# Block-sparse attention in a four-layer fp32 kernel: scores in two halves over 64 rows, queries in two masked forms, full-width transposes

## The reference

```python
Q = heads(x @ W_Q); K = heads(x @ W_K); V = heads(x @ W_V)      # 16 heads of 8 channels
avg_sc = einsum(block means of Q, block means of K), averaged   # blocks of 32 tokens
_, idx = top_k(avg_sc, 3)                                       # 3 key blocks for each query block
logits = einsum('bhtqd,bhtknd->bhtqkn', Qb, Kb[:, :, idx]) / sqrt(8)
P = softmax(logits, axis=-1)                                    # over 3 * 32 = 96 keys
O = einsum('bhtqs,bhtsd->bhtqd', P, Vsel)
```

## Time and profile before

| what | value |
|---|---|
| time, median of 3 runs | 3850.96 us (3844.62 to 3856.63) |
| profiled execution, its own time | 3863.93 us |
| its span, first to last instruction | 3862.0 us |
| busy share of the span: PE, DVE, ACT, POOL | 87%, 60%, 44%, 14% |
| mean granted TensorE clock, share of full speed | 0.895 |
| HBM traffic over the span | 18 GB/s |
| the stage `block_attention` | about 269 to 594 us |

### The profile page before, as it was taken

The page is one execution under the profiler, slowest core; times in us unless marked ns, Lnnn a source line. Parts: engine busy times, 40 slices in busy tenths (PEclk is TensorE's granted clock), DMA queues, the critical chain, the costliest instruction groups (busy, mean ns, idle before and its releaser), DMA issues. The chain is left out here.

```text
span 3862.0 us, 124868 instructions
## 1 busy us (share of the span) xinstructions
PE 3363.0 (87%) x55256; PEld 2074.3 (54%) x55256; DVE 2329.7 (60%) x6283; ACT 1703.4 (44%) x3930; POOL 528.0 (14%) x532
## 2 busy tenths in 40 slices
PE   5866765789999999999989869999999999999985
PEld 2335552335555555455555425666666666666772
DVE  5756663277767777676774115666566666666545
ACT  3657773464444444344332325334444444343323
POOL 1213231000000000000000002222222222222210
PEclk9987677898989889899888879999999999999867
DMA  2000000121111111111000010000000000000000
GB/s 93 0 19 2 1 2 16 59 65 44 46 38 43 42 40 46 35 46 30 19 3 3 1 46 2 2 3 3 2 3 3 3 3 2 3 2 2 3 2 24
DMA packets 37035, 77.16 MB, mean 20 GB/s; under 512 B 7696, under 2 KB 11152, under 8 KB 35472
## 3 DMA queue, kind: packets, MB, share of 16 engines
q1 hardware_dynamic: 36496, 69.17, 5.5%
HBM read 64.83 MB, written 4.33 MB: 18 GB/s over the span
## 5 line engine op out<-in xcount | busy, mean ns | idle before, releaser
L1602 ACT ACTIVATE g_hidden<-ps 128x512 f32<-128x512 f32 x224 | 133.2, 594 | 405.3 <-PE ps L1460 405.1
L1460 PE MATMUL ps<-w_w 128*128 128x512 f32 x448 | 271.3, 690 | 42.7 <-DVE w_w L1810 27.0
L1316 PEld LDWEIGHTS ps<-g_Q,g_K 32*32 32x32 f32 x12288 | 192.6, 113 | 189.0 <-issue 127.3
L2279 PE MATMUL ps<-d_hp,d_w_k 128*128 128x512 f32 x512 | 283.7, 641 | 0.0
L1476 PE MATMUL ps<-g_hidden,w_w 128*128 128x512 f32 x448 | 257.3, 661 | 0.8 <-issue 0.7
L2357 POOL TENSOR_TENSOR d_sq<-d_QK 128x512 f32<-128x512 f32 x128 | 133.1, 1040 | 869.7 <-ACT d_QK L2408 708.4
L2377 ACT ACTIVATE d_F<-ps 128x128 f32<-128x128 f32 x256 | 70.8, 276 | 355.6 <-PE ps L2188 352.4
L1316 PE MATMUL ps<-g_Q,g_K 32*32 32x32 f32 (+1 forms) x12288 | 223.0, 218 | 4.0 <-issue 2.0
L791 ACT ACTIVATE att_p<-ps,att_mx 128x96 f32<-128x96 f32 x512 | 166.0, 361 | 74.6 <-DVE att_mx L736 70.1
L1284 POOL COPY g_xb<-X 128x512 f32<-128x512 f32 x8 | 6.9, 868 | 1191.5 <-DVE X L1822 1091.2
L2552 DVE SCALAR_TENSOR_TENSOR d_conv<-ps,w_conv_q,d_conv 128x511 f32<-128x511 f32 (+2 forms) x192 | 142.3, 741 | 34.1 <-ACT d_conv L2402 30.3
(11 more groups left out here) (502 smaller groups left out, 7877.1 us busy)
## 6 DMA issues: line engine op xcount, KB each, us to landing
w_w<-gate_rows SPq DMA_DIRECT2D x56, 256.0 KB, 3.4
w_w<-in_c_fc_dram SPq DMA_DIRECT2D x56, 256.0 KB, 4.0
w_w<-in_c_proj_dram SPq DMA_DIRECT2D x56, 256.0 KB, 2.8
X<-in_x_dram SPq DMA_DIRECT2D x1, 2048.0 KB, 8.3
w_c_fc<-in_c_fc_dram SPq DMA_DIRECT2D x1, 2048.0 KB, 12.7
w_c_proj<-in_c_proj_dram SPq DMA_DIRECT2D x1, 2048.0 KB, 17.1
ex_root<-gate_rows SPq DMA_DIRECT2D x1, 2048.0 KB, 13.8
h_rows<-k SPq DMA_DIRECT2D x1, 2048.0 KB, 6.3
```

Source lines behind the costliest of these rows:

```text
L1316: ins = e.matmul(later(scored, n_), keys_, queries(n_, planes, r_, 4 * i + j), start=(turn_ == 0 and part == 0 and n_ != 1), stop=(part == 1),
L1460: e.matmul(P[2], fc[:, n % 2, ts(f, C)], hs[n % 2], start=True, stop=True).then_inc(pe.steps, pe.did(now(f"u{i}")))
L1602: e.activation(r[:, slot], P[2], ACT.Relu).then_inc(act.steps, act.did(now(f"r{i}")))
L2279: ins = e.matmul(b, w_k[:, j, ts(H, C)], hp_of(u)[:, j:j + T], start=(j == 0), stop=(j == TAPS - 1))
```

## The change

Scores, maxima and the release of the score banks go by halves. Half h of a unit now has two matrices of scores for each sequence, each from 64 rows (two groups): the queries of the group that is not wanted are masked to zero. For that, `att_qx` becomes two tiles: form 0 keeps the even groups (made by DVE), form 1 the odd ones (made by POOL, `later_queries`), and the scales are a 128 x 8 table. The number of score matmuls stays 16 for a unit; they use two row tiles of 64 rows in place of four of 32. `scores(n+1, half)` waits only for the exponentials of the same half of unit n. The order of PE's and DVE's loops changes. `att_p` gets 128 columns for each matrix, the last 32 zeroed once by DVE, so that the transposes have a 128-column stationary operand. The rings hold three blocks in place of four. The slots of a unit hold the groups in the order 0, 2, 1, 3 (`group_of`).

```diff
...
@@ -668,15 +668,15 @@
 
 
     nc = k.nc
-    NK, BLOCKS, RING = 96, T // 32, 4
+    NK, BLOCKS, RING = 96, T // 32, 3
     UNITS = 2 * BLOCKS
     with ExitStack() as s:
         kg = k.sb("att_kg", [C, RING, B, NK], stack=s)
         vg = k.sb("att_vg", [C, RING, B, NK], stack=s)
-        qx = k.sb("att_qx", [C, RING, B, 4, 32], stack=s)
+        qx = [k.sb(f"att_qx{i}", [C, RING, B, 4, 32], stack=s) for i in range(2)]
         mx = k.sb("att_mx", [C, 2, 16], stack=s)
         den = k.sb("att_den", [C, 2, 16], stack=s)
-        p = k.sb("att_p", [C, 2, 16, NK], stack=s)
+        p = k.sb("att_p", [C, 2, 16, C], stack=s)
         pt = k.sb("att_pt", [NK, 2, 16, C], stack=s)
         vt = k.sb("att_vt", [NK, 2, 4, C], stack=s)
         o = k.sb("att_o", [C, 4, 32], stack=s)
@@ -684,6 +684,8 @@
         scored = k.ps[:, 0:4, 0:4 * NK].rearrange("p g (n k) -> p g n k", k=NK)
         BANK_VT, BANK_PT, BANK_O = 4, 5, 7
         place_of = lambda n: (n // 2, n % 2)
+        group_of = lambda j: 2 * (j % 2) + j // 2
+        scale_of = lambda half, i: k.w["pair_scale"][:, 4 * half + i:4 * half + i + 1]
         last_of = lambda q: 2 * q + 1
         pe, act, dve, pool, dma = k.stage("attention")
         with nc.Block() as block:
@@ -701,46 +703,56 @@
                         j = e.value_load(idx_row[0:1, bass.ds(q * 3 + i, 1)], min_val=0, max_val=15)
                         e.tensor_copy(vg[:, q % RING, :, ts(i, 32)], v1[:, :, bass.ds(j * 32, 32)]).then_inc(pool.steps, pool.did(f"v{q}"))
 
+                def later_queries(q):
+                    if q >= RING:
+                        e.wait_ge(pe.steps, pe.at(f"s{last_of(q - RING)}1"))
+                    for i in range(4):
+                        e.tensor_scalar(qx[1][:, q % RING, :, i, :], q1[:, :, ts(q, 32)], scale_of(1, i),
+                                        None, ALU.mult).then_inc(pool.steps, pool.did(f"q{q}"))
+
                 def weigh(n, g):
-                    w = p[:, n % 2, ts(g, 4)]
+                    w = p[:, n % 2, ts(g, 4), 0:NK]
                     e.wait_ge(dve.steps, dve.at(f"rden{n}{g // 2}"))
                     e.tensor_tensor(w, w, den[:, n % 2, ts(g, 4)].unsqueeze(2).to_broadcast([C, 4, NK]), ALU.mult).then_inc(pool.steps, pool.did(f"p{n}{g}"))
 
                 gather(0)
+                later_queries(0)
+                later_queries(1)
                 for n in range(UNITS):
                     weigh(n, 1)
                     weigh(n, 3)
                     if n % 2 == 0 and n + 2 < UNITS:
                         gather(n // 2 + 1)
+                    if n % 2 and n // 2 + 2 < BLOCKS:
+                        later_queries(n // 2 + 2)
 
             @block.vector
             def _(e):
                 def gather_keys(q):
                     if q >= RING:
-                        e.wait_ge(pe.steps, pe.at(f"s{last_of(q - RING)}"))
+                        e.wait_ge(pe.steps, pe.at(f"s{last_of(q - RING)}1"))
                     for i in range(3):
                         j = e.value_load(idx_row[0:1, bass.ds(q * 3 + i, 1)], min_val=0, max_val=15)
                         e.tensor_copy(kg[:, q % RING, :, ts(i, 32)], k1[:, :, bass.ds(j * 32, 32)]).then_inc(dve.steps, dve.did())
 
                 def gather_queries(q):
                     for i in range(4):
-                        e.tensor_scalar(qx[:, q % RING, :, i, :], q1[:, :, ts(q, 32)], k.w["head_scale"][:, i:i + 1],
+                        e.tensor_scalar(qx[0][:, q % RING, :, i, :], q1[:, :, ts(q, 32)], scale_of(0, i),
                                         None, ALU.mult).then_inc(dve.steps, dve.did(f"q{q}"))
 
-                def maximum(n):
+                def maximum(n, half):
                     if n >= 2:
-                        e.wait_ge(act.steps, act.at(f"exp{n - 2}3"))
-                    e.wait_ge(pe.steps, pe.at(f"s{n}"))
-                    for half in range(2):
-                        m4 = mx[:, n % 2, ts(half, 8)].rearrange("p (g n) -> p g n", g=2)
-                        e.tensor_reduce(m4, scored[:, ts(half, 2)], AX.X, ALU.max, negate=True).then_inc(dve.steps, dve.did(f"max{n}{half}"))
+                        e.wait_ge(act.steps, act.at(f"exp{n - 2}{2 * half + 1}"))
+                    e.wait_ge(pe.steps, pe.at(f"s{n}{half}"))
+                    m4 = mx[:, n % 2, ts(half, 8)].rearrange("p (g n) -> p g n", g=2)
+                    e.tensor_reduce(m4, scored[:, ts(half, 2)], AX.X, ALU.max, negate=True).then_inc(dve.steps, dve.did(f"max{n}{half}"))
 
                 def weigh(n, half):
                     e.wait_ge(act.steps, act.at(f"exp{n}{2 * half + 1}"))
                     e.reciprocal(den[:, n % 2, ts(half, 8)], den[:, n % 2, ts(half, 8)]).then_inc(dve.steps, dve.did(f"rden{n}{half}"))
                     e.wait_ge(dve.steps, dve.n)
                     g = 2 * half
-                    w = p[:, n % 2, ts(g, 4)]
+                    w = p[:, n % 2, ts(g, 4), 0:NK]
                     e.tensor_tensor(w, w, den[:, n % 2, ts(g, 4)].unsqueeze(2).to_broadcast([C, 4, NK]), ALU.mult).then_inc(dve.steps, dve.did(f"p{n}{g}"))
 
                 def keep_values(n):
@@ -760,23 +772,27 @@
                                                ALU.mult, ALU.add).then_inc(dve.steps, dve.did(f"out{n}"))
                     e.wait_ge(dve.steps, dve.n)
 
+                e.memset(p[:, :, :, NK:], 0.0).then_inc(dve.steps, dve.did())
                 gather_keys(0)
                 gather_queries(0)
-                maximum(0)
+                maximum(0, 0)
+                maximum(0, 1)
                 keep_values(0)
                 gather_keys(1)
                 gather_queries(1)
                 for n in range(UNITS):
                     weigh(n, 0)
-                    if n:
-                        pick_heads(n - 1)
-                    weigh(n, 1)
-                    if n + 1 < UNITS:
-                        maximum(n + 1)
-                        keep_values(n + 1)
                     q = n // 2 + 2
                     if q < BLOCKS:
                         (gather_queries if n % 2 else gather_keys)(q)
+                    if n + 1 < UNITS:
+                        maximum(n + 1, 0)
+                    weigh(n, 1)
+                    if n:
+                        pick_heads(n - 1)
+                    if n + 1 < UNITS:
+                        maximum(n + 1, 1)
+                        keep_values(n + 1)
                 pick_heads(UNITS - 1)
 
             @block.scalar
@@ -788,7 +804,7 @@
                     for g in (2 * half, 2 * half + 1):
                         for b in range(4):
                             i = 4 * g + b
-                            e.activation(p[:, n % 2, i, :], scored[:, g, b], ACT.Exp, bias=mx[:, n % 2, i:i + 1],
+                            e.activation(p[:, n % 2, i, 0:NK], scored[:, g, b], ACT.Exp, bias=mx[:, n % 2, i:i + 1],
                                          accum_out=den[:, n % 2, i:i + 1]).then_inc(act.steps, act.did(f"exp{n}{g}"))
 
                 def keep(n, r):
@@ -817,16 +833,18 @@
                         ins = e.transpose(k.ps[0:NK, BANK_VT, ts(b, C)], vg[:, q % RING, 4 * u + b, :], k.w["ident"][:])
                     ins.then_inc(pe.steps, pe.did(f"vt{n}"))
 
-                def scores(n):
+                def scores(n, half):
                     q, u = place_of(n)
                     e.wait_ge(dve.steps, dve.at(f"q{q}"))
                     if n:
-                        e.wait_ge(act.steps, act.at(f"exp{n - 1}3"))
+                        e.wait_ge(act.steps, act.at(f"exp{n - 1}{2 * half + 1}"))
+                    if half:
+                        e.wait_ge(pool.steps, pool.at(f"q{q}"))
                     for b in range(4):
-                        for g in range(4):
-                            ins = e.matmul(scored[:, g, b], qx[ts(g, 32), q % RING, 4 * u + b, :, :].rearrange("p h q -> p (h q)"),
-                                           kg[ts(g, 32), q % RING, 4 * u + b, :], start=True, stop=True, tile_position=(32 * g, 0))
-                    ins.then_inc(pe.steps, pe.did(f"s{n}"))
+                        for r in range(2):
+                            ins = e.matmul(scored[:, 2 * half + r, b], qx[half][ts(r, 64), q % RING, 4 * u + b, :, :].rearrange("p h q -> p (h q)"),
+                                           kg[ts(r, 64), q % RING, 4 * u + b, :], start=True, stop=True, tile_position=(64 * r, 0))
+                    ins.then_inc(pe.steps, pe.did(f"s{n}{half}"))
 
                 def turned(n, r):
                     if r % 2:
@@ -836,7 +854,7 @@
                     if r >= 2 or n:
                         e.wait_ge(act.steps, act.at(f"pt{n}{r - 2}" if r >= 2 else f"pt{n - 1}{r + 2}"))
                     for b in range(4):
-                        ins = e.transpose(k.ps[0:NK, BANK_PT + r % 2, ts(b, C)], p[:, n % 2, 4 * r + b, :], k.w["ident"][:])
```

(25 more changed lines are left out.)

## The result

The changed kernel takes 3787.16 us (median of 4 runs, 3773.09 to 3791.25) against 3852.9 us of the kernel before (median of its 4 runs): ratio 0.9838, 95% interval 0.9812 to 0.9863, 66 us less. The forecast was 3783 us. The profiled execution took 3791.05 us (3863.93 before).

The account below looks back on a forecast made before the run. The prediction took the serial loop of exponentials, scores and first reduction as the bound: (9.83 - 7.4) x 31 = 75 us off, less zeroing, slow start and small waits, net 68, so 3851 - 68 = 3783 us, range 3766 to 3820.

Parts of the forecast that it names:

- The loop is cut: Scores and exponentials: each half's scores need only that half's exponentials, leaving ACT's own period of 6.97 us as floor.
- DVE is the bound by a little: DVE's queue: its work, register loads and small distances sum to about 7.4 us a unit, against ACT at 7.0.
- A half of the scores at the rate of 32-row tiles: PE's scores: each 64-row tile goes at a 32-row tile's rate, 1.08 us a half at full clock, 1.97 at half.
- rival 3: PE's scores: the two 64-row tiles do not overlap, 8.3 us a unit, 3811 us in all; chance 0.08.
- POOL's scaling 0.6 us: POOL's four query scalings per pair of units: 0.6 us each, with bounds of 0.40 and 1.20.
- The clock stays up: PE's clock: with 5.8 us of work in 7.4 it stays full, but for the first units; over 0.9 in the stage.
- rival 1: PE's clock falls now and then, 30 to 50% of units taking 10.5 us: 3804 to 3825 us; chance 0.15.
- Rival 2: PE's queue: the clock stays down and PE is the bound at 10.5 us a unit, 3873 us; chance 0.05.
- Wide transposes for nothing: PE's transposes: loading 128 columns in place of 96 is hidden and costs nothing, at most 0.7 us a unit.
- The sum: The whole stage: 75 us off, 1 back for zeroing, 5 for slow start, 1 to 2 for small waits; net 68.
- Rival 4: DVE slowed beside POOL, or ACT still stands: 0.8 us more a unit, 8.2 us, 3808 us in all; chance 0.10.
- The signs: Profile marks: stage 257 us, unit 7.3 to 7.6, ACT's maxima wait under 25, DVE over 90%, clock over 0.9.

Follow-up runs that it names:

- e1: The changed kernel, but scores of either half wait for all exponentials of the unit before, as before the change: 3958.3 us, ratio 1.0277.
- e3: The changed kernel, but DVE makes both forms of the queries and POOL none: 3780.7 us, ratio 0.9815.
- e4: The changed kernel, but score halves over 32-row tiles with one form of the queries, no scalings on POOL: 3777.0 us, ratio 0.9808.
- e2: The changed kernel, but POOL makes its four scalings two by two, after each of two weighings: 3776.0 us, ratio 0.9800.
- e5: The changed kernel with transposes of 96 columns and no zeroing: 3788.9 us, ratio 0.9853.
- e7: The kernel before the change with only the 128-column transposes and the zeroing: 3845.4 us, ratio 0.9994.
- e11: e4 with one ACT copy moved to DVE, the weighing of slot 2 and later key gathers moved to POOL: 3759.1 us, ratio 0.9755.
- e9: e4 with an extra ACT copy of 0.48 us for a unit, into a tile nobody reads: 3798.3 us, ratio 0.9852.
- e10: e4 with an extra DVE copy of 0.7 us for a unit, into a tile nobody reads: 3808.8 us, ratio 0.9892.

## Why the prediction was right, and where it was not

- **What bounds the kernel now**: right. The loop through all exponentials, scores and first reduction was the bound; the wait of 70.1 us that carried it is 6.8, and e1 shows what the wait costs when it is put back.
- **The loop is cut, ACT's own period of 6.97 us is the floor**: right. The round shown takes 6.95 us at full clock, and two units 14.15, with ACT busy throughout.
- **"DVE is the bound by a little", 7.4 us**: this step failed, by its size. At full clock ACT's own work filled the units without a pause, and a unit took 7.07 us. DVE is close behind: in e3, where it is the bound at full clock, a unit takes 7.63 us with 0.69 of added work, so the changed kernel's DVE needs about 6.95 (an estimate from the two), 0.45 less than the 7.4 summed. About 0.3 of that is busy time (6.99 a unit in e3, so 6.3 without the added work, for the 6.6 summed) and 0.15 is idle time (0.64 for the 0.8 put on top).
- **A half of the scores at the rate of 32-row tiles**: right, 1.07 us from start to start at full clock, and a length of 2.03 at half clock, against 1.08 and 2.04. The two 64-row tiles overlap; rival 3 is out. The Trainium skill (TensorE: Matmul & The Clock Gate, LDWEIGHTS) says that the load's time goes with columns and not with rows: the trace agrees, 187 against 188 ns in e4 and the changed kernel.
- **POOL's scaling 0.6 us**: mis-sized. It is 0.97 on the mean (0.91 at least), inside the bounds of 0.40 and 1.20 and beyond the 0.4 to 0.8 that the prediction gave as the mark. The upper end's consequence, a late weighing that holds PE's queue, came true in every second unit (14 waits of PE's matmuls, 11.6 us in all).
- **The clock stays up**: failed as put, and rival 1 took part. It fell seven times between 290 and 500 us and once more at 501.4, each time after a stretch in which PE was 1.7 to 2.0 of 3.4 us busy and POOL was in its scalings. Each fall lengthened two units, by some 2.6 us together, so the eight cost about 21 us (an estimate from the reductions' starts). e2 took the scalings apart: 9.9 us, clock 0.95. The price of rival 1 was also summed too low: it leaves out the 7 us that the main sum and rivals 3 and 4 give back, with which it would be 3811 to 3832. Rival 2 did not come: where PE was busy without pause at half clock (6.66 of 6.70 us, 405.90 to 412.60), the clock was back at full right after (scores of 1.14 us at 413.13). The Trainium skill (TensorE: Matmul & The Clock Gate, Part 4: PE-mode transpose) says that transposes do not count as busy for the clock in the way that matmuls do, from which the prediction drew a time nearer to rival 2's. The mean clock of 0.89, in a stage with 512 records of these transposes beside 1024 of scores and 1024 of outputs, is not near half for this mixture. No run here has transposes alone.
- **Wide transposes for nothing**: right by e5 and by the times of e7.
- **The sum**: 68 us forecast, 65.7 by the medians, 60.5 in the stage of the profiled pair. The mean unit was 7.8 us in place of 7.4: full-clock units faster than summed (6.9 and 7.2), and units with a fallen clock slower. Two misses of opposite sign, of which the clock's was the larger; that they nearly cancel is luck, and the hit on the total is better than the working behind it.
- **Rival 4, DVE slowed beside POOL**: the slowing was there, its cause was another. Not POOL's longer work made gathers grow but the new order, which puts them beside POOL's weighing (0.76 and 0.92 us for 0.29 and 0.34), as in e3, where POOL has no scalings. It stayed hidden, as DVE at full clock is still 0.1 us behind ACT.
- **The signs**: ACT's wait for the maxima (6.8 us, under 25 asked) and a half of the scores (1.07) came as said. Missed were the stage (264.5 us for 257, by the next stage's first matmul: 535.1 for 595.6), the unit (7.8 for 7.3 to 7.6), the clock (0.89 for over 0.9), DVE's share (178 of 210 us, 85%, and about 90% with its register loads, for over 90%) and POOL's scalings. None of the three signs of being wrong appeared.

## What to carry to other kernels

A wait that covers a whole shared buffer can be split only together with the order of the queues behind it: the halves were worth nothing in the old order, and the new order with the old wait cost 3%. After such a cut, write down for each queue what stands ahead of the instruction that the others wait for; four cheap scalings in one row on an engine with time to spare cost 10 us of distance here (one profile of each) by standing ahead of a weighing. Before a total is read as "this engine was not the bound", look at a stretch in which nothing else changed: e3's total hid that DVE was the bound at full clock. And move work until the fullest engine is full and the others are not late: in e11 PE is 168.7 of 180 us busy, and the clock stays full.

## What the runs showed of the hardware that was not expected

A tensor-by-scalar instruction over 128 x 256 on POOL takes 0.91 us at least, 3.6 ns for an element of a partition, while a two-tensor one over 128 x 384 takes 1.20, 3.1 ns: for an element, reading one tensor less saved nothing, with only these two sizes to go by (spans on POOL are rough: the 14 weighings right behind a row of scalings show as 0.82). DVE's instructions that read one tensor of SBUF grow beside POOL's two-tensor weighing: key copies to 0.81 us at most against 0.29, query scalings to 0.92 against 0.34. Beside POOL's tensor-by-scalar scaling the copy hardly grows (0.31), and the query scaling grows to 0.55. DVE's own two-tensor weighing takes 0.56 beside POOL's weighing in both kernels. The granted clock fell without a long pause: in 402.40 to 405.80 PE was half busy, its longest pause 1.0 us (1.2 for the weight loads), and right after the clock was at half; before the change the fall shown came 1.7 us after the end of a standstill of 3.4 us. The cost of an added instruction can exceed its length (e9, e10: 23 and 31 us for 15 and 22); the clock was lower in both, and how much of the surplus is its part was not isolated.
